# First attention: probabilities turned by the copy, against scores made twice with the keys on partitions

## The chip, the cores and the metric

The kernel runs on one core of a Trainium2 chip. The metric is the device time of one execution in microseconds; the kernel before takes 1097.09 us, the median of three runs (1096.67 to 1097.81). Engines are named as the profile names them: PE (TensorE, matrix products), ACT (ScalarE), DVE (VectorE), POOL (GpSimd) and SP (the queue that issues most DMAs). Products leave PE in PSUM, in banks of 128 partitions x 512 f32 numbers.

## The reference

Two decoder layers on x of 16 sequences x 128 positions x 256 features. Each layer adds an attention, a second mixing step and a feed-forward step to x, each on the layer norm of x. The change touches only the first step:

```
q, k, v = heads(lora_linear(norm(x), W, b, B, A))     # 16 heads of 16 features
scores  = einsum('bhqd,bhkd->bhqk', q, k) * 16**-0.5
attn    = softmax(scores, axis=-1)
out     = einsum('bhqk,bhkd->bhqd', attn, v)          # heads joined to 256 features
x       = x + lora_linear(out, Wo, bo, Bo, Ao)
```

Behind it come a long convolution, an FFN with low-rank experts, a causal attention with 16 heads of 128 features, a linear attention and a mixture of experts. None of that code is changed.

## The kernel before, in words

The program is a list of stages; the first is `stage_lora_attention` (L165). The stage goes through 64 units. A unit n is four heads (s = 0 to 3) of one sequence; four units are a sequence, sixteen a group of four sequences (`U` = 16, `NG` = 4 groups). With x positions on partitions, each group is normalised (DVE, with one operation on POOL for the power -1/2), turned by PE, split into a high and a low part (ACT `hi_chunk`, DVE `lo_chunk`) and projected to q, k and v by `product`, three fp32r products per pair of operands (L41 to L43). q and k lie with the features of four pairs of heads in four 32-row strips; q is kept twice, each copy with the other head of a pair zeroed (`parity`), so a product of 32 rows gives one head's scores.

For a unit, before the change: `scores` (L343) makes scores for two units at a time, queries on partitions, into one bank per unit, four banks in turn. `row_max` (DVE) takes the negated maxima; `exps` (ACT, L508) makes four exponentials of 128x128 with the maximum as bias and the row sum as accumulated output; `inverse_sums` (DVE) takes reciprocals of the four sums; `normalise` (POOL, L275) multiplies 128x512 probabilities by them; `turn` (PE, L353) transposes them into one bank; `keep_probT` (DVE, L581) copies them to SBUF; `weigh` (PE, L365) multiplies by v in four 32-column strips, where the two heads of a pair have their 16 features next to zeros and are added up in the one bank `b_v`. After four units `keep_o` (ACT) and `o_rest` (DVE) split the output in high and low, `project` (PE) applies Wo, and `update` (DVE) adds to x.

The order of the work is written out by hand: every engine runs one loop over n, with offsets such as `STATS_AT`, `HI_AT`, `PROJECT_AT` and `ADD_AT`, and `extra(g, u)` puts a piece of the next group's projections behind unit u of group g. Engines wait on semaphores (`wait_ge`); each runs its own list in order. POOL also adds the output's bias to x and makes 16 products for the convolution (`conv_piece`); DVE adds 16 skip terms (`add_skip`) in the last group.

Of the kernel before, what the change touches and what calls it, by code (L numbers as in the profile page):

```python
# [5 lines left out]
F32 = mybir.dt.float32  # L6
# [158 lines left out]
def stage_lora_attention(pr):  # L165

# [4 lines left out]
    N = NG * U  # L174
    LORA = 0.5
    b_p, b_s, b_t, b_v = banks[0:2], banks[2:6], banks[6], banks[7]
    with ExitStack() as ctx:
# [13 lines left out]
        q = sb("q", [P, 2, 2, DC, GT])  # L191
# [4 lines left out]
        NP, NS = 3, 4  # L196
        negmax = sb("negmax", [P, NS, 4])
        sums = sb("sums", [P, NS, 4])
        rsum = sb("rsum", [P, NS, 4])
        at += 2 * G * H * VW  # L200
        prob, probT = [pr.shared[:, at + 4 * P * n:at + 4 * P * (n + m)].rearrange("p (i s k) -> p i s k", i=m, s=4)
                       for n, m in ((0, NP), (NP, 2))]
# [6 lines left out]
        qb_ok = sem("q_bias_ready")  # L209
# [3 lines left out]
        s_ps, max_ok, exp_ok = sem("scores_in_psum"), sem("negmax_ready"), sem("exps_ready")  # L213
        r_ok, prob_ok = sem("rsum_ready"), sem("probs_ready")
        t_ps, t_ok = sem("probsT_in_psum"), sem("probsT_ready")
        av_ps, ot_hi, ot_lo = sem("oT_in_psum"), sem("oT_hi_ready"), sem("oT_ready")
# [6 lines left out]

        STATS_AT, APPLY_AT, BIAS_AT = 3, 6, 10
        HI_AT, PROJECT_AT, ADD_AT = RG + 1, RG + 3, RG + 4
# [34 lines left out]
        def _(pool):  # L262
            nc.gpsimd.memset(pr.minus_half[:], -0.5).then_inc(pr.const_ok, 1)
            nc.gpsimd.memset(v[:], 0.0).then_inc(v_zero, 1)
            pool.wait_ge(pr.const_ok, 1)

            def add_bias(t, j):
                pool.wait_ge(norm.s_xn, norm.done(t))
                own = x[:, t * G + j, :]
                nc.gpsimd.tensor_tensor(own, own, out_bias[:], ALU.add).then_inc(xb_ok, 1)  # L270

            def normalise(n):
                pool.wait_ge(r_ok, n + 1)
                own = prob[:, n % NP]
                nc.gpsimd.tensor_tensor(own, own, rsum[:, n % NS, :].unsqueeze(2).to_broadcast([P, 4, P]), ALU.mult)\  # L275
                    .then_inc(prob_ok, 1)

            PIECES = [(d, half) for d in range(CONV_C) for half in range(2)]
            FIRST = N - U - len(PIECES)  # L280

            def conv_piece(d, half):
                own = conv_input(pr, 0)[:, half]
# [2133 lines left out]
```

## Time and profile before

| | |
|---|---|
| median of three runs | 1097.09 us (1096.67 to 1097.81) |
| span of the profiled execution | 1105.4 us |
| its mean granted clock | 0.935 of 2.4 GHz |
| PE busy over the span | 986.7 us, 89% |
| DVE, ACT, POOL busy | 647.0, 479.1, 262.6 us |
| loop of the first attention | about 32 to 203.5 us |

One execution was profiled; its own time is its span, 1105.4 us from first to last instruction, which is 8.3 us above the runs' median.
### The profile page before, as it was taken

What the parts mean: (1) busy time and instruction counts of PE and PEld (TensorE: products, weight loads), DVE (VectorE), ACT (ScalarE), POOL (GpSimd) and SP (SyncE); (2) the same over time, 40 slices, a digit from 0 to 9 for tenths busy, and PEclk for the clock granted to TensorE, in tenths of its full rate; (3) what the DMA queues carried; (4) which work ended last, traced back from release to release, by engine and by line L of the source; (5) the groups of instructions that cost most, each with busy time, mean ns of one, the idle gap of its engine ahead of it and who ended that gap; (6) DMA issues with size and microseconds to landing.
All of it is one profiled execution on the core that took longest, in us unless ns stands there. A gap on an engine that the chain in (4) does not pass through costs nothing. (4 is left out here: it accounts for less than half of the span.)

```text
span 1105.4 us, 20085 instructions
## 1 busy us (share of the span) xinstructions
PE 986.7 (89%) x7437; PEld 850.5 (77%) x7437; DVE 647.0 (59%) x1392; ACT 479.1 (43%) x1587; POOL 262.6 (24%) x247
## 2 busy tenths in 40 slices
PE   8898999788855389999999999999999977999977
PEld 6666776688755368888888988889888866777757
DVE  5576667378677834544455445645455455677854
ACT  3576775323234124444444444444444444434521
POOL 3353774244055401111111111111111112011000
PEclk9698996989887689999999999999999999989979
DMA  7000000000053010000000000000000006000002
GB/s 280 2 1 2 1 2 1 21 1 1 1 171 115 19 42 1 1 1 1 0 0 0 0 0 0 0 0 0 1 1 1 1 4 241 1 2 2 2 1 76
DMA packets 10518, 27.56 MB, mean 25 GB/s; under 512 B 1936, under 2 KB 7088, under 8 KB 9808
## 3 DMA queue, kind: packets, MB, share of 16 engines
q1 hardware_dynamic: 9728, 26.42, 6.9%
q8 instruction: 45, 0.74, 0.3%
q10 hardware_dynamic: 720, 0.20, 0.1%
q14 instruction: 25, 0.20, 0.1%
HBM read 24.52 MB, written 2.10 MB: 24 GB/s over the span
## 5 line engine op out<-in xcount | busy, mean ns | idle before, releaser
L1158 POOL TENSOR_TENSOR wa_prob<-wa_prob,wa_rsum 128x512 f32<-128x512 f32 x64 | 66.9, 1045 | 443.6 <-DVE wa_rsum L1375 443.6
L41 PE MATMUL bank<-norm_xT_hi,wide_hi 128*128 128x512 f32 x256 | 106.8, 417 | 2.2 <-ACTq L1342 2.2
L1302 ACT ACTIVATE wa_prob<-wa_prob,wa_negmax 128x128 f32<-128x128 f32 x256 | 100.0, 391 | 17.5 <-DVE wa_negmax L1364 17.2
L1401 DVE TENSOR_TENSOR le_w_or_z_lo<-bank,le_w_or_z_hi 128x512 fp32r<-128x512 f32 x64 | 44.2, 691 | 105.6 <-ACT le_w_or_z_hi L1335 104.9
L43 PE MATMUL bank<-norm_xT_hi,wide_lo 128*128 128x512 f32 x256 | 101.8, 398 | 0.0
L42 PE MATMUL bank<-norm_xT_lo,wide_hi 128*128 128x512 f32 x256 | 101.6, 397 | 0.0
L508 ACT ACTIVATE v_or_conv<-bank,la_negmax 128x128 f32<-128x128 f32 x256 | 90.4, 388 | 6.9 <-PE bank L353 5.1
L1317 ACT COPY wa_v<-bank 128x512 f32<-128x512 f32 x64 | 37.4, 585 | 127.8 <-PE bank L43 127.8
L1310 ACT COPY wa_q<-bank 128x512 f32<-128x512 f32 x64 | 37.5, 586 | 115.6 <-PE bank L43 115.6
L275 POOL TENSOR_TENSOR v_or_conv<-v_or_conv,la_rsum 128x512 f32<-128x512 f32 x64 | 66.4, 1040 | 80.4 <-DVE la_rsum L576 80.3
L1370 DVE COPY wa_k<-bank 128x512 f32<-128x512 f32 x64 | 44.2, 691 | 68.3 <-PE bank L43 68.3
L41 PE MATMUL bank<-wide_hi,le_w_or_z_hi 128*128 128x256 f32 x256 | 73.3, 286 | 1.7 <-DVE le_w_or_z_lo L1401 1.4
L1388 DVE COPY wa_probT<-bank 128x512 f32<-128x512 f32 x64 | 44.1, 688 | 51.3 <-PE bank L1220 51.3
L42 PE MATMUL bank<-wide_lo,le_w_or_z_hi 128*128 128x256 f32 x256 | 71.7, 280 | 0.0
L43 PE MATMUL bank<-wide_hi,le_w_or_z_lo 128*128 128x256 f32 x256 | 71.5, 279 | 0.0
L1230 PEld LDWEIGHTS bank<-wa_probT,wa_v 128*128 128x128 f32 x512 | 65.9, 191 | 7.1 <-DVE wa_probT L1388 2.6
L1230 PE MATMUL bank<-wa_probT,wa_v 128*128 128x128 f32 x512 | 67.9, 275 | 0.7 <-DVE wa_probT L1388 0.7
L1182 PE MATMUL bank<-wa_k,wa_q 128*128 128x128 f32 x512 | 67.6, 275 | 0.0
L132 POOL TENSOR_TENSOR norm_rstd<-norm_rstd,minus_half 128x4 f32<-128x4 f32 x23 | 24.0, 1045 | 179.2 <-DVE norm_rstd L118 179.1
L1182 PEld LDWEIGHTS bank<-wa_k,wa_q 128*128 128x128 f32 x512 | 62.7, 192 | 0.5
L581 DVE COPY v_or_conv<-bank 128x512 f32<-128x512 f32 x64 | 43.9, 686 | 30.6 <-PE bank L353 30.5
L508 ACT ACTIVATION_READ_ACCUMULATOR v_or_conv<-bank,la_negmax 128x1 f32 x256 | 58.3, 228 | 0.0
(282 smaller groups left out, 2567.7 us busy)
## 6 DMA issues: line engine op xcount, KB each, us to landing
le_raw<-in_wide_w SPq DMA_DIRECT2D x16, 512.0 KB, 4.1
em_w<-in_em_w SPq DMA_DIRECT2D x1, 4096.0 KB, 15.4
x<-in_x SPq DMA_DIRECT2D x4, 512.0 KB, 4.7
lc_kt<-in_ctx_rev SPq DMA_DIRECT2D x1, 2048.0 KB, 10.1
lc_toep<-in_toeplitz SPq DMA_DIRECT2D x1, 2048.0 KB, 14.5
out_x<-x SPq DMA_DIRECT2D x8, 256.0 KB, 2.9
li_kt<-in_ctx_rev SPq DMA_DIRECT2D x1, 1536.0 KB, 7.6
la_w_raw<-in_l_w SPq DMA_DIRECT2D x1, 1024.0 KB, 6.4
```

The lines of the kernel that those rows point to most:

```text
L41: nc.tensor.matmul(out, a[0], b[0], start=start, stop=False, skip_group_check=True)
L42: nc.tensor.matmul(out, a[0], b[1], start=False, stop=False, skip_group_check=True)
L43: return nc.tensor.matmul(out, a[1], b[0], start=False, stop=stop, skip_group_check=True)
L275: nc.gpsimd.tensor_tensor(own, own, rsum[:, n % NS, :].unsqueeze(2).to_broadcast([P, 4, P]), ALU.mult)\
L508: last = nc.scalar.activation(prob[:, n % NP, s, :], b_s[n % RG][:, s * P:(s + 1) * P], ACT.Exp, bias=negmax[:, n % NS, s:s + 1], accum_ou ...
L1158: nc.gpsimd.tensor_tensor(prob[:, s], prob[:, s], rsum[:, s, :].unsqueeze(2).to_broadcast([P, G, P]), ALU.mult).then_inc(prob_ok, 1)
L1182: last = nc.tensor.matmul(b_s[s][:, t], q[:, s, t], k[:, s, t], start=True, stop=True)
L1230: last = nc.tensor.matmul(b_z[:, j * P:(j + 1) * P], v[:, g % 2, j, m * HD:(m + 1) * HD], probT[:, h % 2, j, :], start=True, stop=True)
L1302: last = nc.scalar.activation(prob[:, s, j, :], prob[:, s, j, :], ACT.Exp, bias=negmax[:, s, j:j + 1], scale=SCALE, accum_out=sums[:, s, j ...
L1370: nc.vector.tensor_copy(k[:, s, :], b_p[1][:, :]).then_inc(k_ok, 1)
L1388: nc.vector.tensor_copy(probT[:, t % 2], b_t[:, :].rearrange("p (j k) -> p j k", j=G))\
L1401: nc.vector.tensor_tensor(z[1][:, t % 2, :], b_z[:, :], z[0][:, t % 2, :].bitcast(F32), ALU.subtract).then_inc(z_lo, 1)
```

## The change

The scores are computed twice. The first time as before, queries on partitions, only for the maxima. The second time the operands are exchanged (`score_turned`), so that keys are on partitions, in a bank of `b_e`; both heads of a pair in one product of 256 columns. `subtract_max` then adds to that bank, for each head, the product of the negated maxima, spread over 128 columns as weights, with a unit matrix in fp32r: this puts -max(query) in every row. The exponentials are then one ACT instruction of 128x512 per unit, straight into `probT`; nothing is normalised, transposed or copied. `weigh` makes four more products per unit with a matrix of ones and zeros (`ones`), which give the row sums in the layout of the output, in columns 128 to 255 of the bank; two banks `b_v` alternate by pair of units. Per pair, DVE takes the reciprocal of 128x128 sums and multiplies (`divide`); the result goes to SBUF tile `o`, from which `keep_o` and `o_rest` split it. Scores and maxima now alternate between two banks, `phase(p)` issuing scores of pair p interleaved with turned scores and subtraction of pair p-1; weighing runs four units behind. On POOL the bias and the convolution's products stand in one row, since no normalising is between them. A new cast on ACT makes `ident_r`; q's layout changes its order of indices.

```diff
+            def score(n, s):
+                i, own, rows = place(n)
+                m, e = divmod(s, 2)
+                last = nc.tensor.matmul(b_s[n % 2][:, s * P:(s + 1) * P], q[rows, i, m, e, own], k[rows, i, m, own],
+                                        start=True, stop=True)
...
+            def score_turned(n, m):
+                i, own, rows = place(n)
+                nc.tensor.matmul(b_e[n % 2][:, 2 * m * P:2 * (m + 1) * P].rearrange("p (e t) -> p e t", e=2),
+                                 k[rows, i, m, own], q[rows, i, m, :, own], start=(m == 0), stop=False,
+                                 skip_group_check=True)
+
+            def subtract_max(n):
                 for s in range(4):
+                    last = nc.tensor.matmul(b_e[n % 2][:, s * P:(s + 1) * P],
+                                            negmax[:, n % NS, s:s + 1].to_broadcast([P, P]), ident_r[:],
+                                            start=False, stop=(s == 3), skip_group_check=True)
+                last.then_inc(e_ps, 1)
+
+            def phase(p):
+                a = 2 * p
...
+                if 0 < p:
+                    pe.wait_ge(max_ok, a)
+                if 1 < p:
+                    pe.wait_ge(exp_ok, a - 2)
+                for m in range(DC):
+                    for e in range(2):
+                        if p < NPH:
+                            for d in range(2):
+                                score(a + d, 2 * m + e)
+                        if 0 < p and e == 0:
+                            for d in range(2):
+                                score_turned(a - 2 + d, m)
+                if 0 < p:
                     for d in range(2):
...
+                        subtract_max(a - 2 + d)
-            def turn(n):
-                pe.wait_ge(prob_ok, n + 1)
-                wait(pe, t_ok, n)
-                for s in range(4):
-                    last = nc.tensor.transpose(b_t[:, s * P:(s + 1) * P], prob[:, n % NP, s, :], pr.ident[:])
-                last.then_inc(t_ps, 1)
...
                 for s in range(4):
+                    rows = slice(VW * s, VW * s + VW)
+                    last = nc.tensor.matmul(bank[rows, P:2 * P], ones[:, d, :], probT[:, n % NP, s, :],
+                                            start=False, stop=(d == 1), skip_group_check=True)
                 last.then_inc(av_ps, 1)
...
             def exps(n):
 
-                act.wait_ge(max_ok, n + 1)
-                wait(act, t_ps, n - NP + 1)
-                for s in range(4):
-                    last = nc.scalar.activation(prob[:, n % NP, s, :], b_s[n % RG][:, s * P:(s + 1) * P], ACT.Exp,
-                                                bias=negmax[:, n % NS, s:s + 1],
-                                                accum_out=sums[:, n % NS, s:s + 1])
-                last.then_inc(exp_ok, 1)
+                act.wait_ge(e_ps, n + 1)
+                wait(act, av_ps, n - NP + 1)
+                nc.scalar.activation(probT[:, n % NP, :, :], b_e[n % 2][:, :].rearrange("p (s k) -> p s k", s=4),
+                                     ACT.Exp).then_inc(exp_ok, 1)
...
-            def inverse_sums(n):
-                dve.wait_ge(exp_ok, n + 1)
-                nc.vector.reciprocal(rsum[:, n % NS, :], sums[:, n % NS, :]).then_inc(r_ok, 1)
-
-            def keep_probT(n):
-                dve.wait_ge(t_ps, n + 1)
-                wait(dve, av_ps, n - 1)
-                nc.vector.tensor_copy(probT[:, n % 2, :, :], b_t[:, :].rearrange("p (s k) -> p s k", s=4))\
-                    .then_inc(t_ok, 1)
+            def divide(p):
+                b, c = divmod(p, 2)
+                dve.wait_ge(av_ps, 2 * (p + 1))
+                wait(dve, o_ok, p)
+                nc.vector.reciprocal(rsum[:], b_v[p % 2][:, P:2 * P]).then_inc(sum_ok, 1)
+                wait(dve, ot_lo, b - 1)
+                dve.wait_ge(sum_ok, p + 1)
+                nc.vector.tensor_tensor(o[:, b % 2, c, :], b_v[p % 2][:, 0:P], rsum[:], ALU.mult).then_inc(o_ok, 1)
```

On PE, a pair of units in the first group, before; the rows are instructions, x4 a run of four (L353 the turning, L343 the scores, L365 the weighing, L41 to L43 a piece of a projection):

```order
L353 MATMUL bank<-ident,v_or_conv 128x128 x4
L343 MATMUL bank<-la_k,la_q 128x128 x8
L365 MATMUL bank<-v_or_conv 32x128 x4
L353 MATMUL bank<-ident,v_or_conv 128x128 x4
L365 MATMUL bank<-v_or_conv 32x128 x4
L41 MATMUL bank<-la_w_hi,la_oT_hi 128x256
L42 MATMUL bank<-la_w_lo,la_oT_hi 128x256
L43 MATMUL bank<-la_w_hi,la_oT_lo 128x256
```

The same place after the change (L325 scores, L332 turned scores, L338 the subtraction, L377 and L381 the weighing by v and by ones):

```order
L325 MATMUL bank<-la_k,la_q 128x128 x2
L332 MATMUL bank<-la_q,la_k 128x256 x2
L325 MATMUL bank<-la_k,la_q 128x128 x4
L332 MATMUL bank<-la_q,la_k 128x256 x2
L325 MATMUL bank<-la_k,la_q 128x128 x2
L338 MATMUL bank<-la_ident_r,la_negmax 128x128 x8
L377 MATMUL bank<-v_or_conv 32x128 x4
L381 MATMUL bank<-v_or_conv,la_ones 32x128 x4
L377 MATMUL bank<-v_or_conv 32x128 x4
L381 MATMUL bank<-v_or_conv,la_ones 32x128 x4
L41 MATMUL bank<-la_w_hi,la_oT_hi 128x256
L42 MATMUL bank<-la_w_lo,la_oT_hi 128x256
```

Two runs of transposes are gone; turned scores stand between the scores, and all scoring and subtracting is ahead of both weighings.

On DVE, a stretch of the first group before (L576 reciprocal of sums, L571 maxima, L581 the copy of turned probabilities, L586 the low part of the output, L592 the update of x):

```order
L592 TENSOR_TENSOR x<-bank,x 128x256
L576 RECIPROCAL la_rsum<-la_sums 128x4
L571 TENSOR_REDUCE la_negmax<-bank 128x4
L586 TENSOR_TENSOR la_oT_lo<-bank,la_oT_hi 128x256
L581 COPY v_or_conv<-bank 128x512
L576 RECIPROCAL la_rsum<-la_sums 128x4
L571 TENSOR_REDUCE la_negmax<-bank 128x4
L581 COPY v_or_conv<-bank 128x512
L576 RECIPROCAL la_rsum<-la_sums 128x4
```

And after (L584 maxima, L591 and L594 the division, L604 the update, L598 the low part):

```order
L584 TENSOR_REDUCE la_negmax<-bank 128x4 x2
L591 RECIPROCAL la_rsum<-bank 128x128
L594 TENSOR_TENSOR la_o<-bank,la_rsum 128x128
L584 TENSOR_REDUCE la_negmax<-bank 128x4 x2
L591 RECIPROCAL la_rsum<-bank 128x128
L594 TENSOR_TENSOR la_o<-bank,la_rsum 128x128
L604 TENSOR_TENSOR x<-bank,x 128x256
L148 TENSOR_TENSOR la_xT_lo<-bank,la_xT_hi 128x512
L598 TENSOR_TENSOR la_oT_lo<-la_o,la_oT_hi 128x256
L584 TENSOR_REDUCE la_negmax<-bank 128x4 x2
```

The maxima of two units now stand together, the reciprocal is of 128x128 numbers, and the update of x stands behind a division.

## Rows read from the trace of the kernel before

**Rows 1.** The stretches view, one per group of four sequences: each engine's busy us, (x) instructions.
```profile
core 0: us, PE busy (x) PEld busy (x) DVE busy (x) ACT busy (x) POOL busy (x), PEclk, DMA share, GB/s
32.10:78.00 45.90, 42.31 (x387) 31.99 (x388) 29.60 (x72) 29.96 (x142) 20.79 (x22) 0.83 0.01 2
78.00:122.30 44.30, 39.66 (x403) 30.21 (x402) 29.28 (x73) 30.46 (x144) 20.41 (x22) 0.92 0.01 2
122.30:161.80 39.50, 36.46 (x399) 27.65 (x398) 25.80 (x57) 29.91 (x143) 30.10 (x37) 1.00 0.01 1
161.80:203.50 41.70, 35.35 (x328) 25.11 (x326) 30.35 (x84) 22.63 (x119) 16.11 (x16) 0.75 0.01 2
```

**Rows 2.** The same view, cut where the granted clock changes, and at full clock.
```profile
27.50:30.90 3.40, 2.02 (x36) 1.66 (x34) 1.52 (x4) 2.24 (x13) 0.00 (x0) 1.00 0.02 5
30.90:41.20 10.30, 9.09 (x46) 6.96 (x46) 5.29 (x11) 5.58 (x26) 4.16 (x4) 0.50 0.00 1
144.00:161.80 17.80, 16.60 (x191) 12.95 (x189) 11.97 (x28) 12.72 (x67) 14.91 (x21) 1.00 0.00 1
170.90:174.30 3.40, 1.45 (x20) 0.82 (x18) 3.37 (x12) 1.98 (x10) 2.70 (x3) 1.00 0.00 0
174.30:194.80 20.50, 19.94 (x143) 14.55 (x144) 13.68 (x35) 10.48 (x57) 7.68 (x8) 0.50 0.00 1
```

**Rows 3.** The timeline of PE, group 2: start us, us, engine, line, tiles, records.
```profile
141.39 0.28 PE L43 MATMUL bank<-la_w_hi,la_oT_lo 128*128 128x256 f32 x1
...
141.86 0.40 PE L41 MATMUL bank<-la_xT_hi,la_w_hi 128*128 128x512 f32 x1
142.09 0.39 PE L42 MATMUL bank<-la_xT_lo,la_w_hi 128*128 128x512 f32 x1
...
142.70 0.63 PE L353 MATMUL bank<-ident,v_or_conv 128*128 128x128 f32 x4
143.26 1.16 PE L343 MATMUL bank<-la_k,la_q 32*128 32x128 f32 x16
144.35 0.43 PE L365 MATMUL bank<-v_or_conv 128*32 128x128 f32 x8
144.71 0.66 PE L353 MATMUL bank<-ident,v_or_conv 128*128 128x128 f32 x4
```

**Rows 4.** The timeline of PE in the linear attention, at full clock.
```profile
1006.82 1.90 PE L1613 MATMUL bank<-li_va,li_kp 128*128 128x64 f32 x16
1008.64 0.73 PE L1603 MATMUL bank<-li_wf,li_kT 32*128 32x128 f32 x16
...
1010.48 1.08 PE L1626 MATMUL bank<-li_qp,li_kv 128*32 128x128 f32 x32
1011.49 0.50 PE L41 MATMUL bank<-norm_xT_hi,li_w_hi 128*128 128x512 f32 x1
```

**Rows 5.** The waits from 30 to 205 us: us in total, times, longest us.
```profile
PEld bank L353 <- POOL v_or_conv L275: 10.3, 11, 2.1
...
PE bank L365 <- DVE la_oT_lo L586: 9.0, 12, 1.4
PE bank L353 <- POOL v_or_conv L275: 8.3, 5, 2.6
```

**Rows 6.** DVE's groups of instructions by shape, whole span: busy us, mean ns, idle before.
```profile
L571 DVE TENSOR_REDUCE la_negmax<-bank 128x4 f32<-128x512 f32 x64 | 42.4, 664 | 7.1 <-PE bank L343 7.1
L1841 DVE RECIPROCAL li_rden<-li_den 128x256 f32<-128x256 f32 x16 | 28.0, 1750 | 12.1 <-ACT li_den L1765 12.1
...
L576 DVE RECIPROCAL la_rsum<-la_sums 128x4 f32<-128x4 f32 x64 | 11.1, 174 | 19.3 <-ACT v_or_conv L508 18.4
...
L687 DVE SCALAR_TENSOR_TENSOR lc_toep<-lc_anti,lc_skip,lc_toep 128x128 f32<-128x128 f32 x16 | 5.7, 359 | 0.0
```

**Rows 7.** ACT's groups of instructions by shape, whole span.
```profile
L508 ACT ACTIVATE v_or_conv<-bank,la_negmax 128x128 f32<-128x128 f32 x256 | 90.4, 388 | 6.9 <-PE bank L353 5.1 <-DVE la_negmax L571 1.7
...
L144 ACT CAST norm_xT_hi<-bank 128x512 fp32r<-128x512 f32 x28 | 15.8, 591 | 33.2 <-PE bank L137 33.1
```

More of the change, by code:

```diff
@@ L263, in _, with add_bias @@
             nc.gpsimd.memset(pr.minus_half[:], -0.5).then_inc(pr.const_ok, 1)
+            nc.gpsimd.memset(ones[:], 0.0).then_inc(v_zero, 1)
             nc.gpsimd.memset(v[:], 0.0).then_inc(v_zero, 1)
+            pool.wait_ge(v_zero, 1)
+            for e in range(2):
+                nc.gpsimd.memset(ones[:, e, e * HD:(e + 1) * HD], 1.0).then_inc(v_zero, 1)
             pool.wait_ge(pr.const_ok, 1)
-            def add_bias(t, j):
+            def add_bias(t):
                 pool.wait_ge(norm.s_xn, norm.done(t))
[L269 to L280, printed above, removed]
+                for j in range(G):
+                    own = x[:, t * G + j, :]
+                    nc.gpsimd.tensor_tensor(own, own, out_bias[:], ALU.add).then_inc(xb_ok, 1)
             def conv_piece(d, half):
@@ L328, in turn_x @@
                 norm.turn_chunk(pe, t, c, bank)
-            def scores(n):
-                t = n // U
-                if n % U == 0:
-                    pe.wait_ge(q_ok, DC * (t + 1))
-                    pe.wait_ge(k_ok, DC * (t + 1))
-                for d in range(2):
-                    wait(pe, exp_ok, n + d - RG + 1)
-                for s in range(4):
-                    m, e = divmod(s, 2)
-                    for d in range(2):
-                        j, r = divmod((n + d) % U, RG)
-                        rows = slice(32 * r, 32 * r + 32)
-                        last = nc.tensor.matmul(b_s[r][:, s * P:(s + 1) * P],
-                                                q[rows, t % 2, e, m, j * P:(j + 1) * P],
-                                                k[rows, t % 2, m, j * P:(j + 1) * P], start=True, stop=True)
-                        if s == 3:
-                            last.then_inc(s_ps, 1)
@@ L359, in weigh @@
                 j, r = divmod(n % U, RG)
[L360 removed]
+                p, d = divmod(n, 2)
+                bank = b_v[p % 2]
+                pe.wait_ge(exp_ok, n + 1)
                 if r == 0:
                     pe.wait_ge(v_ok, 2 * t + j // 2 + 1)
[L363 removed]
+                if d == 0:
+                    wait(pe, o_ok, p - 1)
                 for s in range(4):
[L365 to L367 removed]
+                    rows = slice(VW * s, VW * s + VW)
+                    nc.tensor.matmul(bank[rows, 0:P], v[:, t % 2, j, head(r, s), :], probT[:, n % NP, s, :],
+                                     start=(d == 0), stop=(d == 1), skip_group_check=True)
+                for s in range(4):
+                    rows = slice(VW * s, VW * s + VW)
+                    last = nc.tensor.matmul(bank[rows, P:2 * P], ones[:, d, :], probT[:, n % NP, s, :],
+                                            start=False, stop=(d == 1), skip_group_check=True)
                 last.then_inc(av_ps, 1)
@@ L483, in keep_q @@
                 for e in range(2):
-                    last = nc.scalar.activation(q[:, t % 2, e, m, :], bank[:, :], ACT.Identity,
+                    last = nc.scalar.activation(q[:, t % 2, m, e, :], bank[:, :], ACT.Identity,
                                                 bias=q_bias[:, e, m:m + 1], scale=parity[:, e:e + 1])
```

154 lines of the change are left out of this document (79 added, 75 removed).

## Prediction

> **What bounds the kernel now.** I read four views, in this order. First the stretches by group of four sequences: the first attention's loop of 64 units (a unit is four heads of one sequence) runs from 32.1 us, the first turning of probabilities, to 203.5 us, and its four groups take 45.9, 44.3, 39.5 and, up to the last turning at 199.2 us, 37.4 us, 167.1 together [rows 1]. PE shows 36 to 42 us busy in each group, DVE 26 to 30, ACT 23 to 30, POOL 16 to 30. Second the same view cut at the clock's changes: the groups differ for a reason that is not their work. The granted clock is 0.50 from 30.9 to 41.2 and from 174.3 to 194.8 us (and in two further stretches of 6.8 us, as the means 0.83 and 0.92 say), and ahead of each fall PE was thin: 2.02 us busy of 3.4, and 1.45 of 3.4. Between 144 and 161.8 us, with 16.6 of 17.8 busy, it stayed at 1.00 [rows 1, 2]. 0.50 is 1.2 GHz and 1.00 is 2.4. Third the timeline of one pair of units at full clock, for what PE needs; fourth the waits, for what makes it thin: PE waits for POOL's normalising and for the low part of the output (one PSUM bank holds the output, so weighing can't go on until it is read), 18.6 and 9.0 us, and a serial chain lies behind each unit: sums, reciprocal, POOL, turning, copy, weighing [rows 5]. So the bound is mixed: PE at full clock for most of groups 0 to 2, the chain and the low clock it brings in group 3 and at the start.
>
> **The change on PE, per pair of units at full clock.** Before: a turning takes 0.56 us from its start to the scores' (142.70 to 143.26), the two units' scores 1.09 (to 144.35), a weighing 0.36 (to 144.71), changes of array shape included [rows 3]. A pair is 2 x 0.56 + 1.09 + 2 x 0.36 = 2.93.
>
> After, four items. (1) Scores again, 8 products of 128 columns. (2) Turned scores, 4 products of 256 columns. They use row groups 2 and 3 when the scores use 0 and 1 (and the reverse), write other banks, and stand between the scores in the program. Four row groups do run side by side: 16 records in 0.73 us, while 16 records in two row groups take 1.16 [rows 3, 4]. The turned part is 8 records of double length in two groups, as long as the scores beside it, so it fits under the same 1.09; wholly behind it, it would cost 0.9 more. I take 1.09, since the row nearest in kind shows the overlap. (3) The subtraction: 8 products of 128 columns in fp32r, each with its own 128x128 weights. No row has that form. From below: fp32r takes 0.11 to 0.12 for 256 columns [rows 3], so 0.055 if only columns counted. Nearest: 16 records that move just 64 columns take 1.90 us, (1.90 - 0.28)/15 = 0.108 apiece, 0.28 being the length of the last record (the row at 141.39 shows one) [rows 3, 4], as long as 128 columns; the weights set it. From above: an f32 product, two records, 0.22. I take 0.109 (as the 0.11 of the turnings): 8 x 0.109 + 0.1 for the change of shape = 0.97 (0.54 to 1.86). (4) Weighing and sums by ones, 32 records in four column groups: one row has exactly that, 1.01 from start to the next start [rows 4]. Together 3.07, and about 0.1 more where another product splits the pair: 3.17, 0.24 more than before, or about 2 us per group of eight pairs.
>
> In the Trainium skill, TensorE: Matmul & The Clock Gate, The mechanism (Part 3) speaks against item 3: a weight load overlaps running products only when the row group differs. By that rule load and columns would be paid one after the other; the result is rival A2 below. The trace disagrees: 128-row products of 64 columns keep 0.108 [rows 4], and the 128-row turnings of 128 columns keep (0.63 - 0.28)/3 = 0.12 [rows 3], where a serial load would make the second dearer by half.
>
> **What else PE does in a group.** The projections of the next group are 24 products of 512 columns at 0.23 (141.86 to 142.09) and 24 of 256 at 0.115; the output projection is another 24 of 256, the transposes 8 of 0.11: 5.5 + 2.8 + 2.8 + 0.9 = 12, and 1 for changes of shape: 13 [rows 3]. Demand per group is 8 x 2.93 + 13 = 36.4 before, against 39.5 measured at full clock in group 2: 3.1 of waits. After: 8 x 3.17 + 13 = 38.4.
>
> **What it removes.** 64 normalisings on POOL, 64 reciprocals of four numbers, 64 copies of 128x512 and 256 of the 0.39 us exponentials; an exponential of 128x512 costs nearer 0.6 (the cast of that shape, 0.59) [rows 6, 7], so ACT falls from 1.5 us a unit (4 x 0.39) to 0.6. The waits for POOL and for the single output bank go (18.6 + 9.0).
>
> **What is late next.** DVE's maxima now serve two units at once (2 x 0.66), followed in the same round by the division. Its reciprocal has 128 numbers; 4 take 0.174 and 256 take 1.75 [rows 6], a line between them gives 0.94 (bounds 0.17 and 1.75); with the product, 0.3, and the wait between them, 1.3. So an update of x (256 columns; 0.4, between the skip term's 0.36 for 128 and the maxima's 0.66 for 512) is done 1.33 + 1.3 + 0.4 = 3.0 us after the scores, when PE has had its 0.97 + 1.01 and wants that bank for the projections: about 1.1 us, at two places a group. The output projection waits 0.8 for the low part; at the group's start the transposed x passes ACT (0.59) and DVE (0.66 at this size) with only half a microsecond of weighing beside it: 1.0, and 0.7 for the values' bank. Sum 4.7 per group, 43.1 us in all. Two new waits stand ahead of work that others need. PE waits at each round of scores for the maxima and exponentials of the round before, with the weighings queued behind it; both are done about 1.6 us after the scores' end and the subtraction's end (2 x 0.66 on DVE, 2 x 0.6 on ACT, hand-offs), against PE's 1.98 and 1.01 there, so only the second can cost, some 0.3 in pairs with nothing else between, four or so a group, and I leave it within the range. ACT's cast of the output waits for the division, with exponentials behind it, one per sequence. No other queue is passed: POOL does bias, reciprocal roots and the 16 convolution pieces early and unwaited.
>
> In group 3 nothing is projected but the output: PE needs 8 x 3.07 + 2.8 = 27.4 and DVE, per pair, 1.33 + 1.3 + 0.4 + two skip terms of 0.36 = 3.75, 30 us. DVE sets it: 30.
>
> **The clock.** Part of the gain rests on it. With no unit waiting for POOL, PE has no thin stretch like those of [rows 2] except the start, where two rounds of scores precede the first exponentials. I take full clock from the first weighing on. The Trainium skill, in TensorE: Matmul & The Clock Gate, PE-mode transpose (Part 4), holds that transposes do not count as PE activity; that would favour the change too, which drops 256. The trace can't confirm it: 144 to 161.8 us kept 1.00 with transposes in every unit [rows 2].
>
> **The sum.** Loop: 3 x 43.1 + 30 = 159.3 against 167.1: -7.8. Start: the first unit's turning was at 32.1 and its first weighing will be near 32.5: +0.4. End: from the last unit to the last update 4.3 us before (199.2 to 203.5); now weighing, division, cast, remainder, projection, update: 0.5 + 1.5 + 0.5 + 0.5 + 1.0 + 0.6 = 4.6, and a last unit more in steady pace, +1.1 in all. -6.3. The profiled execution has a span of 1105.4; less 6.3 it would be 1099. It is 8.3 above the runs' median, so I carry over the difference, not the level: 1097.1 - 6.3 = **1091**.
>
> **Rivals.** (A) *The subtraction is dear.* If fp32r at 128 columns costs like f32, 0.22, each pair has 0.89 more. In groups 0 to 2 that is 21 us; in group 3 PE needs 34.5 instead of DVE's 30, 4 more. 1091 + 25, less some 4 of waits that vanish behind it: 1112. For it: no row moves 128 columns in fp32r. Against: 0.115 for 256 shows no such cost at twice the size. It decides from 0.135 apiece: there 32 x 8 x 0.026 = 6.6 us eat the gain. (A2) *The weights of the subtraction load in series with its columns*, 0.109 + 0.055 = 0.16 apiece: 32 x 8 x 0.055 = 14 us, 1105. Against it stand the two pitches of item 3's paragraph. It is what the Trainium skill's section on the mechanism of packing would make of these products. (B) *The clock falls as often as before*, 44 us at half: PE then does 22 us less in its work, 4 to 22 later according to how many of the four stretches recur: 1095 to 1113, slower for three or more. For it: the 4.7 us of waits per group gather at its start, 1.7 in a row with shape changes about them. Against: 1.7 is less than the thin stretches show. (C) *The turned scores don't hide*, 0.9 a pair: 32 x 0.9 = 29, less hidden waits: 1115. (D) *The waits for DVE don't appear* (DVE fast enough, or banks free): 3 x 3 us less: 1082. With the subtraction at 0.055 besides, 3 x 3.5 more off: 1072. (E) *Nothing to see*: the gain in clock is there, and waits of 2 us more a group pay it back: 1097.
>
> **How the numbers follow.** Forecast 0.44, at 1086 to 1096; A 0.10; A2 0.04; B 0.14; C 0.06; D 0.14; E 0.08. A measurement of this kernel tells about 0.2%, 2.2 us, from no change. Faster: 0.42 of the forecast, D's 0.14, 0.02 of B: 0.58. Same: E, 0.02 of the forecast, 0.03 of B: 0.13. Slower: A, A2, C, 0.09 of B: 0.29. The range from 1077 to 1111 leaves out half of A, C, the tail of B and that of D, some 0.19. The likeliest case's own is 1086 to 1096.
>
> **What would show it.** The line of the subtraction at a pitch near 0.11 (A: 0.2); the turned scores starting within 0.02 us of the scores before them (C: behind them); DVE's reciprocal near 0.95; a clock of 1.00 through group 3 and a pair there every 3.8 us; groups 0 to 2 near 43 us. Wrong would be: low clock in group 3, POOL or ACT in a wait of PE, or a long conv stage that changes.

## The result, and the profile after

The changed kernel takes 1112.53 us (median of 4 runs, 1111.36 to 1113.43), the kernel before 1096.88 (4 runs, 1096.30 to 1097.81): ratio 1.0129, 95% interval 1.0104 to 1.0154. It is 15.6 us slower; 1091 was forecast, and the range ended at 1111. Six executions among the timed runs of this and the next sections were over 1.5% longer than the fastest of their kernel and stand in no ratio: 1172.7 us in after_wide46, 1421.0 in before_fill, and 1111.2, 1111.4, 1111.7 and 2376.8 us of the kernel before.

The profile doesn't look like that. Its span is 1109.5 against 1105.4, and the stage that was changed did nearly all that the forecast said. The stretches view by group, from the first weighing on (columns as in [rows 1], which these rows answer):

```profile
35.00:77.30 42.30, 39.07 (x587) 31.97 (x586) 24.76 (x52) 15.36 (x30) 3.80 (x5) 1.00 0.01 2
77.30:121.70 44.40, 40.07 (x598) 32.81 (x599) 27.21 (x57) 16.41 (x33) 15.12 (x21) 1.00 0.01 2
121.70:164.70 43.00, 38.92 (x593) 32.29 (x592) 23.16 (x42) 15.71 (x32) 0.00 (x0) 1.00 0.01 2
164.70:189.20 24.50, 23.19 (x443) 20.01 (x446) 23.69 (x61) 9.30 (x20) 1.05 (x1) 1.00 0.01 3
```

Groups of 42.3, 44.4 and 43.0 us (43.1 forecast), 24.5 for the last, and the clock at 1.00 throughout, where [rows 1] had 0.83, 0.92, 1.00 and 0.75. The timeline of PE for one pair of units (answers to [rows 3]):

```profile
126.58 0.38 PE L325 MATMUL bank<-la_k,la_q 32*128 32x128 f32 x2
126.59 0.48 PE L332 MATMUL bank<-la_q,la_k 32*128 32x256 f32 x2
...
127.35 0.39 PE L325 MATMUL bank<-la_k,la_q 32*128 32x128 f32 x4
127.67 1.11 PE L338 MATMUL bank<-la_ident_r,la_negmax 128*128 128x128 f32 x8
128.71 0.43 PE L377 MATMUL bank<-v_or_conv 128*32 128x128 f32 x8
...
129.72 0.39 PE L41 MATMUL bank<-la_w_hi,la_oT_hi 128*128 128x256 f32 x1
```

Scores L325 and turned scores L332 start 0.01 us apart and take 1.09 together; the eight subtractions take 1.04 to the next start; weighing and sums 1.01. 3.14 a pair, 3.17 forecast. DVE's and ACT's groups of instructions by shape, 35 to 189 us, answer to [rows 6, 7]:

```profile
L584 DVE TENSOR_REDUCE la_negmax<-bank 128x4 fp32r<-128x512 f32 x59 | 38.0, 685 | 46.8 <-PE bank L325 46.8
L522 ACT ACTIVATE v_or_conv<-bank 128x512 f32<-128x512 f32 x62 | 35.9, 600 | 86.3 <-PE bank L338 86.0
L591 DVE RECIPROCAL la_rsum<-bank 128x128 f32<-128x128 f32 x30 | 28.4, 947 | 0.0
L594 DVE TENSOR_TENSOR la_o<-bank,la_rsum 128x128 f32<-128x128 f32 x30 | 8.8, 292 | 2.8
```

So the next stage starts 8.9 us earlier. The first product of the convolution, before and after:

```profile
205.03 0.85 PE L772 MATMUL bank<-v_or_conv,lc_toep 128*128 128x144 f32 x2 [1.68 <-ACTq L831]
```
```profile
196.11 0.85 PE L783 MATMUL bank<-v_or_conv,lc_toep 128*128 128x144 f32 x2 [1.68 <-ACTq L842]
```

The gain is given back three stages later, behind the convolution and the experts, in code that the change doesn't touch. The wide attention is a loop. Its second and third pass by the stretches view, before and then after (the sum is over all four passes):

```profile
525.20:651.90 126.70, 126.63 (x809) 112.95 (x808) 64.02 (x133) 55.41 (x178) 17.73 (x17) 1.00 0.00 0
651.90:778.60 126.70, 126.63 (x809) 112.95 (x808) 64.03 (x133) 55.41 (x178) 17.73 (x17) 1.00 0.00 0
...
sum 502.80, PE 499.15 PEld 444.62 DVE 252.97 ACT 219.69 POOL 70.93; mean PE 124.79 PEld 111.16 DVE 63.24 ACT 54.92 POOL 17.73
```
```profile
519.70:651.50 131.80, 128.70 (x809) 114.10 (x808) 64.12 (x133) 55.22 (x178) 17.75 (x17) 0.99 0.00 1
651.50:784.70 133.20, 129.84 (x809) 115.25 (x808) 64.10 (x133) 55.33 (x178) 17.75 (x17) 0.97 0.00 1
...
sum 514.20, PE 504.45 PEld 448.11 DVE 253.27 ACT 219.38 POOL 71.01; mean PE 126.11 PEld 112.03 DVE 63.32 ACT 54.84 POOL 17.75
```

The same instructions take 514.2 us in place of 502.8: +11.4. The timeline of PE after shows where: at the jump back to the loop's start it waits for nothing that the profile shows ("issue"), twice.

```profile
530.21 0.27 PE L43 MATMUL bank<-wide_hi,le_w_or_z_lo 128*128 128x256 f32 x1
531.60 0.60 PE L1193 MATMUL bank<-wa_k,wa_q 128*128 128x128 f32 x3 [1.12 <-issue]
534.11 0.82 PE L1193 MATMUL bank<-wa_k,wa_q 128*128 128x128 f32 x5 [1.91 <-issue]
```

The page's DMA queues point to the cause, in the row of the queue that brings instructions (packets, MB, share), before and after:

```profile
q8 instruction: 45, 0.74, 0.3%
```
```profile
q8 instruction: 69, 1.13, 0.4%
```

24 more packets of 16 KB. Six of them are the longer program (768 more matmul records and as many weight loads); the other 18 are nine for each of two passes, which before fetched none. The stalls are 3.0 us in the second pass and 3.3 in the third; behind them the clock is at its low level for 3.4 and 6.8 us, where products of 512 columns start every 0.43 us in place of 0.23, which costs some 1.5 and 3.1 us. That is 4.5 and 6.4 of the 5.1 and 6.5 us by which the two passes are longer.

That leaves a riddle. The two profiles differ by 4.1 us, the timed runs by 15.6. In every run listed with both figures the time is the span and 1.8 to 2.2 us, so the profiled execution of before (span 1105.4, granted clock 0.935) took some 1107, 10 more than the runs it was meant to stand for.

### The profile page after: what moved, and what is told of

Read it like the earlier page. It is cut to its first block and busy times, and to the rows that moved or that the text cites. A ratio compares the mean times of both kernels' runs of the same rounds, so it can differ in the third digit from the quotient of the medians.

```text
span 1109.5 us, 21059 instructions
## 1 busy us (share of the span) xinstructions
PE 985.4 (89%) x8205; PEld 861.7 (78%) x8205; DVE 637.2 (57%) x1328; ACT 422.5 (38%) x1140; POOL 197.6 (18%) x186
## 5 line engine op out<-in xcount | busy, mean ns | idle before, releaser
L41 PE MATMUL bank<-norm_xT_hi,wide_hi 128*128 128x512 f32 x256 | 108.1, 422 | 2.2 <-ACTq L1353 2.2
L43 PE MATMUL bank<-norm_xT_hi,wide_lo 128*128 128x512 f32 x256 | 103.4, 404 | 0.0
L41 PE MATMUL bank<-wide_hi,le_w_or_z_hi 128*128 128x256 f32 x256 | 73.2, 286 | 1.7 <-DVE le_w_or_z_lo L1412 1.4
L584 DVE TENSOR_REDUCE la_negmax<-bank 128x4 fp32r<-128x512 f32 x64 | 41.2, 685 | 53.7 <-PE bank L325 53.7
L43 PE MATMUL bank<-wide_hi,le_w_or_z_lo 128*128 128x256 f32 x256 | 71.5, 279 | 0.0
L522 ACT ACTIVATE v_or_conv<-bank 128x512 f32<-128x512 f32 x64 | 37.0, 600 | 88.3 <-PE bank L338 88.0
L43 PEld LDWEIGHTS bank<-norm_xT_hi,wide_lo 128*128 128x128 f32 x256 | 49.4, 193 | 11.9
L41 PEld LDWEIGHTS bank<-norm_xT_hi,wide_hi 128*128 128x128 f32 x256 | 49.5, 193 | 11.7 <-issue 2.5
```

Source lines behind the costliest of these rows:

```text
L41: nc.tensor.matmul(out, a[0], b[0], start=start, stop=False, skip_group_check=True)
L43: return nc.tensor.matmul(out, a[1], b[0], start=False, stop=stop, skip_group_check=True)
L584: nc.vector.tensor_reduce(negmax[:, n % NS, :], b_s[n % 2][:, :].rearrange("p (s k) -> p s k", s=4), AX, ALU.max, negate=True).then_inc(ma ...
```

## Experiments

My theory: (1) the place of the wide loop in PE's instruction memory decides whether it is kept between passes, and the change moved it; (2) the kernel before loses the clock in the first attention in some executions only, the profiled one among them, so most of the "gain" was never there to have. Rivals: the long stretch at full clock makes the chip slower later; or the first attention leaves something behind. Ratios are to the kernel before on the same chip, whose medians go from 1100.0 to 1103.4 on the four chips of these runs; differences in us are between medians, at times of two chips.

**Moving the loop.** The change makes PE's program ahead of the wide attention longer by six blocks of 256 instructions less 46, so the loop (1707 instructions by the program; 809 products and 808 loads of weights of them show in the trace) lies elsewhere within its blocks. Fillers move it back: a filler is a wait for a count long reached, and two such waits make one instruction. In PE's program, ahead of the wide attention:

```
+ for _ in range(92):                    # two waits make one instruction: 46
+     pe.wait_ge(norm.s_lo, DC * norm.split(0))
  qk(0, 0, 0)
```
after_wide46: 

> The changed kernel with 46 more instructions on PE (waits for a semaphore that is already reached) just ahead of the wide attention's loop; the change took 46 instructions net, beside whole blocks of 256, out of PE's program ahead of that loop. Theory 'place': the loop of 1707 instructions now lies over one more 16 KB block than PE keeps, so it is fetched again in each pass, 11 us; with the 46 back it is kept: no instruction packet in its second and third pass, passes of 126.7 us as before, the first attention's 8.9 us stay: 1112.5 - 11 to 1096.9 - 8.9, so 1088 to 1101. Rival 'clock': the first attention at full clock all through leaves the chip fewer fast cycles later, whatever lies where: 1112 to 1114, passes of 132 to 133 us. Rival 'memory': the changed first attention leaves SBUF, PSUM or queues otherwise, same numbers as 'clock'.

Measured: 1106.60 us, ratio 1.0041 (1.0016 to 1.0066), passes of 126.7, no packet in the second and third. The passes are as the theory said; the time is above its 1088 to 1101, since the fillers cost more than I had thought and since the 8.9 us are not gained against most runs of the kernel before (both below).

before_wide90, the same edit with 180 waits in the kernel before: 

> The kernel before, with 90 more such waits at the same place; its first attention is untouched. 
```profile
540.56 1.15 PE L1182 MATMUL bank<-wa_k,wa_q 128*128 128x128 f32 x8 [0.90 <-issue]
```

Most of its extra time is the fillers' own, which I had put far too low: from the experts' last turning to the first score are 33.1 us in place of 23.1, 0.11 each. That the time lies in the expected range is luck: the passes cost less and the fillers more.

before_wide30: 

> The kernel before with 30 such waits there: the price of the waits themselves. Theory 'place': before lies 0 to 45 instructions into a block and may lie up to 85 in, so 30 more change nothing: 1097 to 1099, no packet in the second and third pass. If any shift costs (or the waits do), 1100 and more.

Measured: 1100.13, ratio 1.0004 (0.9969 to 1.0040), 45 packets, passes of 126.7. A shift by 30 keeps the loop; the level above 1099 is that of the kernel before on this chip, 1100.88.

after_start46, the fillers behind PE's very first wait: 

> The changed kernel with the 46 waits at the very start of PE's program instead, where it waits for the first load: every later PE instruction lies in its block as in the kernel before, those of the first attention too. Theory 'place': as with the waits ahead of the wide loop, 1088 to 1101; if it is faster than that by more than 2 us, the place also matters in the stages between. Rivals: 1112 to 1114.

Measured: 1106.13, ratio 1.0033 (0.9999 to 1.0067), passes of 126.7; PE's first product starts at 8.6 us in place of 3.8. So the cure costs 4.8 of what it saves; the time is again above the 1088 to 1101 of the theory. So the fillers went where PE is idle for 14.5 us:

```
+ for _ in range(92):
+     pe.wait_ge(main_ok, 1)
  turn(0)                                # expert stage
```
after_free46: 

> The changed kernel with the 46 filler waits in the expert stage, where PE is idle for 14.5 us before it turns hw: there they cost nothing (the 46 cost about 4.8 us at the two other places, 0.105 each). Theory: place alone, so passes of 126.7 us, no packet in the second and third pass, and some 4.8 us less than the kernels with the 46 elsewhere (1106.1 and 1106.6): about 1101 to 1102, and 11 less than the changed kernel. What stands against a gain then: the kernel before runs the first attention faster in most runs than in its profiled one (a lower clock there), so the gain of 8.9 us in its first attention is not there in most runs: ratio to before 0.998 to 1.003. Rival: the first attention's gain is real in all runs: ratio 0.990 to 0.994.

Measured: 1102.91, ratio 1.0026 (1.0009 to 1.0043), as the theory said; the rival's 0.990 to 0.994 falls. Stretches view of its second pass:

```profile
518.50:645.20 126.70, 126.63 (x810) 112.95 (x809) 64.07 (x133) 55.41 (x178) 17.73 (x17) 1.00 0.00 0
```

before_free210: 

> The kernel before with 210 filler waits in PE's idle stretches of the expert stage (24 ahead of its first product, 35 in its loop, 138 ahead of the turning of hw, 13 ahead of the last transposes), which cost nothing there and put the wide attention's loop just where it lies in the changed kernel (210 = 256 - 46). Theory 'place': passes of 132 to 133 us as in the changed kernel, +11 us: about 1109 to 1112, with the first attention of before. If the extra comes from what the first attention leaves behind and not from the place: 1098 to 1101 and passes of 126.7.

Measured: 1109.82, ratio 1.0078 (1.0051 to 1.0106). Second pass and packets:

```profile
520.10:652.10 132.00, 128.60 (x809) 114.25 (x808) 64.15 (x133) 55.17 (x178) 17.73 (x17) 0.99 0.00 1
```
```profile
q8 instruction: 64, 1.05, 0.4%
```

Nothing of the change is in that kernel but the place of its loop, and the passes take 132.0. For the 11 us of the wide attention both rivals fall. A little of the first may stand: from the convolution's first product to its last, the five profiles of the kernel before have 101.9 to 102.2 us, the five of the changed one 103.2 to 104.6, and so have two profiles of the kernel before whose first attention ran at full clock nearly all through (before_fill, below: 104.3 in both); turned_behind, below, low from 35 to 45 us, has 102.2. Why it is so, no run shows. after_again, the changed kernel on another chip: 

> The changed kernel unchanged, on the chip of these comparisons. Expected: 9 to 11 us above the same kernel with its wide loop in place (1102.9 there, ratio 1.0026 to before): ratio 1.011 to 1.014, about 1112, and a spread under 3 us.

Measured: 1112.72, as on the first chip, but the ratio is 1.0086 (1.0053 to 1.0120), below what I expected: it is the kernel before that differs, 1103.44 there. The spread under 3 us didn't come either: its 11 runs go from 1108.5 to 1116.0.

**The kernel before has no one time.** before_again: 

> The kernel before once more, unchanged, for a second profile. Its runs range from 1095 to 1111 us with a mean granted clock from 0.949 down to 0.929, so the profiled execution (span 1105.4, clock 0.935) was one of the longer. Theory: where this one has a higher clock, it is in the first attention (162 to 205 us above all) that it is higher, and the next stage starts before 200 us in place of 205.0. Rival: the runs differ elsewhere, and the next stage starts at 205 in each.

Measured: span 1101.3, and the first product of the convolution (compare 205.03 above):

```profile
193.82 0.85 PE L772 MATMUL bank<-v_or_conv,lc_toep 128*128 128x144 f32 x2 [1.68 <-ACTq L831]
```

The same code, 11.2 us earlier. Its stretches by group, to be held against [rows 1]:

```profile
30.90:41.20 10.30, 9.74 (x85) 7.06 (x85) 5.93 (x13) 7.80 (x37) 3.85 (x5) 0.83 0.00 1
41.20:78.50 37.30, 32.02 (x338) 24.50 (x338) 26.52 (x67) 26.79 (x131) 18.95 (x20) 0.95 0.01 2
78.50:119.90 41.40, 36.95 (x400) 28.09 (x401) 29.27 (x73) 30.55 (x145) 22.18 (x23) 1.00 0.01 2
119.90:158.40 38.50, 35.97 (x392) 27.19 (x392) 25.38 (x58) 29.12 (x143) 28.20 (x35) 1.00 0.01 2
158.40:189.90 31.50, 27.04 (x284) 19.24 (x288) 26.76 (x74) 18.87 (x103) 14.64 (x15) 0.84 0.01 2
```

30.9 to 41.2 us ran at 0.83 where the first profile had 0.50, the second group at 1.00 for 0.92, the last stretch at 0.84 for 0.75. Twice the length times what the mean clock lacks is the time at the low level: 17 us, against 44 in [rows 1]. Over five profiles of this first attention the convolution starts at 193.8, 196.9, 198.6, 205.0 and 205.4; over the five of the changed one at 194.1, 194.6, 196.1, 196.4 and, with the fillers at the start, 197.8; in all of these the clock is at 1.00 from 36 to 187 us. In 101 runs of the kernel before on four chips (the one of 2376.8 us left out) the time goes from 1094.4 to 1111.7 with its mean clock from 0.949 to 0.929 (correlation -0.91); 12 of after_free46 lie within 3.0 us.

The rival isn't refuted, though: the runs differ elsewhere too. before_again took 1103.1 us, more than the median of 1100.0 on its chip, for 7.1 of its 11.2 us are lost again, against the first profile: 2.7 between the convolution's last product and the wide attention's first scores, 1.6 in the wide attention and 3.0 behind it, each time with more low clock. No execution of the kernel before at 1097 us was profiled. That it is one with its first attention near 194 us and the later stages as short as in the first profile (1105.4 - 11.2 is a span of 1094.2, so a time of some 1096) is put together from two profiles, not seen in one.

before_fill gives PE needless products where it was thin (the lines are shortened):

```
+ fill(b_v[:, :], 8)       # ahead of the first scores, 10 more behind them
+ if t < 3: fill(b_p[0][:, :], 6)              # unit 3 of groups 0 and 1
+ if 3 * U < n < N - 1: fill(b_p[0][:, :], 2)  # 14 units of group 3
```

> The kernel before with 58 needless products of 512 columns on PE (fp32r, into banks that nobody reads then): 18 about the first two rounds of scores, 6 each in unit 3 of groups 0 and 1, two after each unit of group 3; 140 filler waits in the expert stage bring the shift of the later code to 256. Theory: what the kernel before loses now and then is the low clock after thin stretches of PE; with these filled the clock stays at 1.00 and though PE has 13 us more work, the next stage starts at 188 to 194 us in every run and the mean clock is 0.945 or more: 1094 to 1099, at most half the spread of the kernel before. Rival: the low clock comes whatever PE does there, and the products only add: 1103 to 1110, with the same spread (clock 0.93 to 0.945).

Measured: 1100.65, ratio 0.9958 (0.9924 to 0.9992); mean clock 0.951 to 0.955 in 7 of 11 runs, the others at 0.940 to 0.943. The loop of the first attention in its profile:

```profile
30.90:191.30 160.40, 148.45 (x1548) 111.22 (x1548) 115.22 (x285) 115.57 (x563) 88.46 (x95) 0.99 0.01 2
```

before_fill_again: 

> The kernel before with the 58 needless products once more, beside the others on one chip. Expected as measured: ratio 0.992 to 0.999, mean clock 0.950 to 0.955 in most runs.

Measured: 1100.64, ratio 0.9989 (0.9954 to 1.0024), again two clusters of clock, 0.951 to 0.955 and 0.940 to 0.944. In the first attention the products did what I expected: its clock is 0.99 in both profiles, and the convolution starts at 195.4 and 193.9, though PE has 13 us more work. So in this stage the low clock does go with PE's thin stretches. The mean clock of the upper cluster is above that of all 101 runs of the kernel before; but the time gains little, and the halved spread didn't come (1096.3 to 1107.8). The two profiles are one of each cluster, with spans of 1106.0 and 1097.3, and only 1.5 of these 8.7 us are in the first attention: the rest comes from the stages behind the convolution, and so, by these two, do the clusters.

**The terms of the sum.** The subtraction in f32, two records each:

```
- negmax = sb("negmax", [P, NS, 4], F32R)
+ negmax = sb("negmax", [P, NS, 4])
```
free46_sub_f32 (this line, and `pr.ident` for `ident_r` in the product): 

> As after_free46, with the maxima and the unit matrix of the subtraction in f32, so each product is two records with two loads of weights: the subtraction doubles (PE's program grows by 512 instructions, two whole blocks, so no place changes). Theory: PE and its waits both matter: the subtraction goes from 0.109 to 0.22 apiece, 8 x 0.11 = 0.9 a pair, some 21 us in the first three groups and 0 to 4 in the last: 1116 to 1126, groups of 48 to 50 us. Rival: the groups are bound by DVE's chain and PE's extra time vanishes in its waits: under 8 us more, groups under 45.

Measured: 1124.53, ratio 1.0215 (1.0187 to 1.0244), 21.6 above after_free46 on the same chip; sixteen records of the subtraction take 2.05 us, groups last 47.7, 48.5, 47.6 and 28.6. This is rival A come true, and its price was 21.

turned_behind: 

> As after_free46, with the turned scores of a pair behind its scores, not between them. Theory (the four row groups run side by side, so between them the turned scores are free): 0.9 us more a pair while PE sets the pace, 24 pairs, less some waits that vanish: 16 to 20 us more, 1119 to 1123, groups of 48 to 50; in group 3 up to 3 more. Rival (C of the prediction: they were never hidden): 1101 to 1104.

Measured: 1118.43, ratio 1.0137 (1.0075 to 1.0200), 15.5 above after_free46; groups 48.8 (with the clock at 0.92), 47.0, 45.7 and 26.1. A pair's scores and the start of its subtraction:

```profile
102.14 0.82 PE L325 MATMUL bank<-la_k,la_q 32*128 32x128 f32 x10
...
103.76 1.10 PE L338 MATMUL bank<-la_ident_r,la_negmax 128*128 128x128 f32 x8
```

1.62 us, where the changed kernel has 1.09 (126.58 to 127.67 above). Between the scores the turned ones are hidden, as forecast, and rival C is refuted. Part still overlaps when they stand behind: they cost 0.5 a pair, not 0.9, and the two middle groups, at full clock, are 2.7 us longer, not 7; some of PE's waits vanish behind them. In the profile the first rounds cost 2.5 us more and the clock is low from 35 to 45 us, which is most of the rest.

update_early, DVE's order alone:

```
- HI_AT, PROJECT_AT, ADD_AT = RG + 5, RG + 7, RG + 8
+ HI_AT, PROJECT_AT, ADD_AT = RG + 5, RG + 7, RG + 7
```

> As after_free46, with DVE's update of x one unit earlier in its program, in the unit of its projection: ahead of the next pair's maxima and of the division, where it stood behind both. Theory: the waits for DVE that the prediction put at 1.1 us at two places a group (PE wants the bank that the update reads) vanish, and nothing else is late for it: 5 us less in the first three groups, 42.4, 44.3 and 43.0 become 40.5 to 42.5 each: 1102.9 - 5 = 1098, 1096 to 1100. Rival (the waits only move to the division or the low part of the output): 1101 to 1104.

Measured: 1099.24, 3.7 below after_free46, ratio 0.9955 (0.9927 to 0.9983), which is 0.7% below that of after_free46: the two were timed on different chips. PE's waits for the update of x, 4.9 us in after_free46, are gone; groups 41.4, 42.2 and 40.8, and 25.8 for the last; of the waits, 1.7 us came back as waits for maxima and the low part.

diag174, in short:

```
+ nc.gpsimd.tensor_tensor(diag[:, n % 2], <ident, 4 times>, <negmax of 4 heads>, ALU.mult)
- for s in range(4): matmul(b_e[n % 2][:, s * P:(s + 1) * P], <negmax s>, ident_r[:], ...)
+ matmul(b_e[n % 2][:, :], <ones>, <diag, 512 columns>, ...)
```

> The changed kernel with the subtraction made otherwise: POOL, idle in the changed kernel, multiplies the unit matrix by each head's maxima (128x512, as large as the normalising before), and one product of 512 columns with a matrix of ones as weights subtracts all four heads: 0.23 us a unit in place of 4 x 0.109. The bias of x and the convolution pieces go back between POOL's units, the output before splitting moves to a free part of the shared tile, and 174 filler waits in the expert stage keep the wide loop's place. Theory (PE sets groups 0 to 2, DVE group 3): 8 x 0.41 = 3.3 us less PE work a group, waits up by 0.8, so groups of 40 to 41 in place of 42.4, 44.3 and 43.0 and 24 to 25 for the last; the start 1.2 later: 1102.9 - 6 = 1097, 1094 to 1100. Rival (the chain through DVE, now with POOL in it, sets the groups): groups of 43 to 46, 1103 to 1110.

Measured: 1104.41, ratio 1.0015 (0.9985 to 1.0046); groups 40.6, 44.7, 41.7, 25.1. Between theory and rival: the clock fell once in group 1 (mean 0.96), and PE waited 6.7 us for the update. With both edits, diag_update_early: 

> Both edits: the subtraction by POOL's diagonal matrices and the early update. In the kernel with the diagonal alone PE waited 6.7 us for the update of x, more than without it (4.9). Theory: these go, 7 us less: groups of 38 to 41, and 1104.4 - 7 = 1097, 1094 to 1100. Rival (the chain over DVE and POOL sets the groups): 1102 to 1105.

Measured: 1097.31, ratio 0.9940 (0.9911 to 0.9969), the lowest ratio of all; beside it the kernel before had 1103.44 and the changed one 1112.72. Its groups:

```profile
34.40:73.50 39.10, 36.07 (x539) 26.59 (x538) 25.75 (x53) 15.40 (x30) 20.23 (x21) 1.00 0.01 2
73.50:114.20 40.70, 37.51 (x545) 27.62 (x544) 27.88 (x58) 16.53 (x33) 23.53 (x25) 1.00 0.01 2
114.20:152.90 38.70, 36.08 (x545) 27.02 (x547) 24.69 (x41) 15.63 (x32) 27.28 (x33) 1.00 0.01 2
152.90:178.90 26.00, 21.59 (x407) 16.16 (x410) 24.85 (x60) 9.68 (x20) 13.25 (x13) 1.00 0.01 3
```

## Why the prediction was wrong

**The steps inside the stage held.** A pair on PE takes 3.14 us (3.17 forecast); the subtraction 0.109 to 0.115 from start to start (0.164 behind the first of eight), so rivals A and A2 fall. With A2 falls, for these products, the rule that the prediction quotes from the Trainium skill (TensorE: Matmul & The Clock Gate, The mechanism (Part 3)). The turned scores are hidden; reciprocal 0.947 (0.94), product 0.292 (0.3), exponential 0.600 (0.6); groups 43.1 forecast, 42.3 to 44.4 found; full clock from the first weighing, so not B. The waits for DVE at the bank were real too (update_early). Low was only the last group: 24.5 to the last unit, where I had 30 by DVE and 27.4 by PE. Measured are 23.7 us of DVE and 23.2 of PE: both sums counted eight whole pairs, but when the last group's weighing starts, part of its scores and maxima is made (the window has 11 of 16 maxima). The convolution started at 196.1, and my sum said 205.0 - 6.3 = 198.7.

**What failed is the last line of the sum:** "I carry over the difference, not the level: 1097.1 - 6.3". It holds two assumptions, and each was wrong by more than the whole forecast.

- *That nothing outside the stage moves.* The change moves the wide loop within its blocks of instructions. That is +11.4 us in the profile; 0.6 to 1.0% between after_free46 (1.0026) and the changed kernel (1.0129 on one chip, 1.0086 on another), and +9.8 us when the kernel before is moved so. No rival of mine had it.
- *That the profiled difference is that of ordinary runs.* I had seen that the profile of before lay 8.3 us above the runs' median, and put it down to the level. It was, for the most part, in the very thing that the gain rested on: 44 us of low clock, where another execution has 17 and is through the stage 11.2 us earlier. I also took 0.2% for what these runs can tell apart, from three runs within 1.2 us; over 101 runs the kernel before varies by 17 us.

Behind both stands a third point: at full clock the change gains nothing. The middle groups take 44.4 and 43.0 us, where the kernel before takes 41.4 and 38.5 (before_again), as 38.4 of demand and 4.7 of waits against 36.4 and 3.1 had said. Only the last one is shorter: 24.5 for 31.5 in before_again, of which 10 us are low, and for 28.9 in before_wide90, the quickest that it was in a profile:

```profile
165.60:194.50 28.90, 24.33 (x280) 17.14 (x280) 26.24 (x74) 18.61 (x102) 14.58 (x15) 0.94 0.01 2
```

The quickest groups of the unfilled kernel before, put together, are some 152 us (43.3 in before_free210, the 41.4, 38.5 and 28.9 above), those of the changed one 154.2. So the forecast gain was low clock avoided, and an execution that has little of it gains nothing.

Together: forecast -6.3; the stage itself 2.6 better than that; +11.4 for the loop; +11.2 for a first attention of before that is already at 193.8. That is +13.7, and +15.6 was measured. In the two profiles the other stretches add 1.6: 1.5 in the convolution (103.7 for 102.1), 2.1 up to the wide attention, -2.0 behind it. The +11.2 is the term that rests on least: it takes the first attention of one execution and the rest of another. And the four runs that the result compares with (1096.3 to 1097.8) were quick ones: on the four chips of the later runs the median is 1100.0 to 1103.4, and beside 1103.44 the changed kernel was 9.3 us slower, not 15.6.

What stays open: why the kernel before loses the clock in the first attention in one execution and not in the next, where the same instructions run; what makes the stages behind the convolution vary (behind the wide attention 200 to 204 us in the kernel before, 199 to 204 in the changed one); and from which shift on the loop is lost (30 keeps it, 90 and 210 don't). The low price of before_wide90 (1.2 us a pass) and the high one of before_free210 (5.3) come from two places of the same loop: one stall of 0.9 at full clock against two of 3.2 together and 3.4 us of low clock; why there is a second stall is open. The Trainium skill (Runtime: NRT & Kernel Launch, Instruction fetch mechanics) gives PE an instruction memory of 2048 instructions, refilled in blocks of 256, and says that a taken branch to a block that isn't there stalls. By that, as an estimate, a loop of 1707 instructions fits if it lies over seven blocks and one is being fetched ahead, and no longer over eight: the runs agree, with the nine packets a pass and the two stalls at the jump, but none tries the edge between the two. The same section says that only two blocks are held and fetching is purely sequential; the trace disagrees: the kernel before jumps back over 1707 instructions and fetches nothing.

## What to carry to other kernels

A change in one stage moves the instructions of all later ones: compare the packets of the instruction queue, and look for a loop that fetches in every pass, before you believe a slowdown or a gain. A filler instruction is free only where the engine is idle. And before a gain is read from a profile, hold that execution's time against the timed runs: if it differs by as much as the gain, find out in which stage, since what you mean to cure may be what happened in that execution alone.

## What the runs showed of the hardware

- An instruction that waits for counts long reached costs PE 0.105 to 0.11 us (4.8 us for 46, 10.0 for 90), not the 0.02 to 0.06 that I had assumed.
- A loop's place is worth 1.2 to 6.5 us in a pass of 127 us: 0.8 to 2.5 in one stall, and in the dear place products of 512 columns at 0.43 us in place of 0.23 for 3.4 to 6.8 us behind it (mean clock 0.97 and 0.99 in passes that had 1.00).
- The low clock comes to the same instructions in one execution and not in the next: 17 to 44 us of it in a first attention that ends at 194 to 205 us, in five profiles. Needless products in its thin stretches bring that to 4 us in both profiles taken. The changed kernel has none there in any of five; even so its runs repeat only within 2 to 7.5 us.
- Products with their own 128x128 weights follow each other at 0.11 us with 128 columns in fp32r. In f32 each is two records, 0.22 us (2.05 us for eight with the first's surplus). POOL's product of 128x512 with two broadcast operands takes 1.04 us, as the normalising did.
